# Attention's softmax within batches of 64 nodes, and attention and token mixing by 64x64 blocks of TensorE's array

## The reference, cut to what matters

```
layer 0:  agg = einsum('nm,bmd->bnd', A_hat, x);  two linear layers with batch norm
layer 1:  xp  = einsum('mn,bnf->bmf', L_norm, x);  h = relu(layernorm(xp @ Wc + bc)) + x
          q, k, v: 4 heads of 64;  scores = q k^T / 8, where(adj > 0, scores, -1e9)
          o = softmax(scores) @ v;  layernorm(x1 + o @ Wo);  MLP of 512 with gelu
layer 2:  h = relu(einsum('ts,bsh->bth', adj, x @ Wg0 + bg0));  h = relu(einsum(..., h @ Wg1 + bg1))
          then LSTMs over windows of 1 to 4 nodes (10 cells)
layer 3:  graph attention, softmax over the nodes of a batch
```

## Time and profile before

| | us |
|---|---|
| median of 3 runs | 2272.82 (2272.42 to 2273.76) |
| profiled execution | 2277.71 |
| its span | 2275.9 |
| PE busy | 2078.6 (91%) |
| DVE busy | 1650.3 (73%) |
| ACT busy | 1363.2 (60%) |
| POOL busy | 201.5 (9%) |

### The profile page before, as it was taken

The page is one execution under the profiler, slowest core; times in us unless marked ns, Lnnn a source line. Parts: engine busy times, 40 slices in busy tenths (PEclk is TensorE's granted clock), DMA queues, the critical chain, the costliest instruction groups (busy, mean ns, idle before and its releaser), DMA issues.

```text
span 2275.9 us, 56395 instructions
## 1 busy us (share of the span) xinstructions
PE 2078.6 (91%) x21545; PEld 1786.0 (78%) x21545; DVE 1650.3 (73%) x4811; ACT 1363.2 (60%) x3393; POOL 201.5 (9%) x260
## 2 busy tenths in 40 slices
PE   7989669999899999999999989999999999999986
PEld 4544358889788988888888978898889888888875
DVE  5769556777777777777677877777777777777744
ACT  5547335666565756666566656575657566666653
POOL 2000010010101010101010110001010101010100
PEclk9989779999999999999999999999999999999997
DMA  7747200000100001000100010001000010000000
GB/s 272 268 168 270 78 10 11 11 11 2 39 2 20 2 2 40 11 11 2 40 11 11 2 39 11 11 2 32 10 11 11 2 40 11 11 2 11 2 11 10
DMA packets 36751, 86.39 MB, mean 38 GB/s; under 512 B 2416, under 2 KB 26992, under 8 KB 32752
## 3 DMA queue, kind: packets, MB, share of 16 engines
q1 hardware_dynamic: 36464, 82.56, 10.4%
HBM read 52.15 MB, written 30.41 MB: 36 GB/s over the span
## 4 chain that ended last, share of the span: by engine, by line
PE 33%; DVE 22%; issue 19%; ACT 10%; POOL 5%; DVEq 0%; ACTq 0%; POOLq 0%
PE ps L257 9%; PE ps L258 9%; PE ps L259 9%; POOL rstd L1505 5%; DVE stats L1546 3%; ACT pool_mem L1379 2%; DVE pool_mem L1692 2%; ACT pool_mem L1413 2%; DVE pool_mem L1676 1%; PE ps L1092 1%; DVE pool_mem L1678 1%; ACT pool_mem L1421 1%; DVE mv L1550 1%; DVE hl_a L1598 1%; DVE hl_b L1598 1%
## 5 line engine op out<-in xcount | busy, mean ns | idle before, releaser
L1413 ACT ACTIVATE pool_mem<-ps,lstm_b 128x128 f32<-128x128 f32 (+2 forms) x1248 | 438.1, 415 | 289.8 <-PE ps L259 273.3
L257 PE MATMUL ps<-hl_a,w_hi 128*128 128x256 f16 (+2 forms) x1984 | 469.8, 260 | 21.7 <-DVE hl_a L776 8.0
L258 PE MATMUL ps<-hl_a,w_hi 128*128 128x256 f16 (+2 forms) x1984 | 469.2, 260 | 0.0
L259 PE MATMUL ps<-hl_a,w_lo 128*128 128x256 f16 (+2 forms) x1984 | 469.2, 260 | 0.0
L257 PE MATMUL ps<-hl_b,w_hi 128*128 128x168 f16 (+2 forms) x1408 | 361.9, 265 | 21.3 <-issue 17.0
L258 PE MATMUL ps<-hl_b,w_hi 128*128 128x168 f16 (+2 forms) x1408 | 361.4, 265 | 0.0
L259 PE MATMUL ps<-hl_b,w_lo 128*128 128x168 f16 (+2 forms) x1408 | 360.9, 265 | 0.0
L1505 POOL TENSOR_TENSOR rstd<-ve,nhalf 128x2 f32<-128x2 f32 x224 | 184.2, 825 | 1834.9 <-DVE ve L1553 1834.9
L257 PE MATMUL ps<-pool_mem,w_hi 128*128 128x128 f16 (+2 forms) x1536 | 313.0, 234 | 0.7
L258 PE MATMUL ps<-pool_mem,w_hi 128*128 128x128 f16 (+2 forms) x1536 | 312.9, 234 | 0.0
L259 PE MATMUL ps<-pool_mem,w_lo 128*128 128x128 f16 (+2 forms) x1536 | 312.8, 234 | 0.0
(11 more groups left out here) (246 smaller groups left out, 4587.4 us busy)
## 6 DMA issues: line engine op xcount, KB each, us to landing
xa<-in_x SPq DMA_DIRECT2D x32, 512.0 KB, 4.8
h_scratch<-pool_mem SPq DMA_DIRECT2D x14, 1024.0 KB, 4.2
pool_mem<-h_scratch SPq DMA_DIRECT2D x14, 1024.0 KB, 6.4
pool_mem<-in_wpack SPq DMA_DIRECT2D x16, 704.0 KB, 4.1
out<-xb SPq DMA_DIRECT2D x16, 512.0 KB, 2.9
o_scratch<-act_in SPq DMA_DIRECT2D x14, 512.0 KB, 3.2
act_in<-o_scratch SPq DMA_DIRECT2D x14, 512.0 KB, 5.6
row<-in_rows SPq DMA_DIRECT2D x1, 1408.0 KB, 10.2
```

The costliest lines, as they stand in the source:

```text
L257: nc.tensor.matmul(o, l[0], r[0], start=first, stop=False, skip_group_check=True)
L258: nc.tensor.matmul(o, l[0], r[1], start=False, stop=False, skip_group_check=True)
L259: return nc.tensor.matmul(o, l[1], r[0], start=False, stop=last, skip_group_check=True)
L1413: op = nc.scalar.activation(gates[s][:, g, m * w:(m + 1) * w], ps[s][:, g, m * w:(m + 1) * w], ACT.Tanh, bias=lstm_b[:, bias:bias + 1], sc ...
```

## The change

1. Softmax is computed within a batch only. The mask is 128x64. The scores of a half are 16 matmuls of 64x64x64 that use the two diagonal quadrants of the array (partitions 0 to 63 into 0 to 63, 64 to 127 into 64 to 127) and fill one bank. DVE adds the mask, takes the minimum of each row and subtracts it in three operations of 512 columns; ACT takes one exponential; DVE sums, inverts and scales. There are 4 transposes and one copy.
2. Attend is 16 matmuls of 64x64x64 in all four quadrants of the array, one bank for each batch of a block.
3. `mix` and `aggregate` go through a new function `quarters`: instead of one matmul with a block-diagonal matrix, four with its 64x64 block, in the four quadrants, one bank for each batch. ACT's and DVE's splits read two banks through a view; the number of elements is the same.
4. Banks: the gcn's first product moves to another bank, and the second one waits for the low half of half 0 too.
The list of the round is not changed, nor is the order of the steps on any engine. `pe.sem_inc(begun, 1)` is a semaphore increment on PE ahead of each such group.

```diff
+        def quarters(to, of, matrix):
+            for f in range(KT):
+                for c in (slice(0, P // 2), slice(P // 2, P)):
+                    for batch in range(P // NODES):
+                        n = slice(batch * NODES, (batch + 1) * NODES)
+                        mm = nc.tensor.matmul(to(f, batch)[c, :], of(f)[n, c], matrix[n, n], start=True, stop=True)
+            return mm
...
-                nc.gpsimd.tensor_scalar(mask1[:, :], a_bd[:, :], 0.0, MASK_L1, ALU.is_le, ALU.mult).then_inc(set_ok, 1)
+                for b in range(P // NODES):
+                    pool.wait_ge(set_ok, b + 1)
+                    d = slice(b * NODES, (b + 1) * NODES)
+                    nc.gpsimd.tensor_scalar(mask1[d, :], a_bd[d, d], 0.0, MASK_L1, ALU.is_le, ALU.mult).then_inc(set_ok, 1)
...
                 def aggregate(s, n):
-                    for f in range(KT):
-                        for b in range(BLK):
-                            mm = nc.tensor.matmul(ps[s][:, f, b * P:(b + 1) * P], xa[s][:, b, f * P:(f + 1) * P],
-                                                  gcn_t[:, :], start=True, stop=True)
+                    pe.sem_inc(begun, 1)
+                    for b in range(BLK):
+                        mm = quarters(lambda f, batch: ps[s][:, batch, (f * BLK + b) * NODES:(f * BLK + b + 1) * NODES],
+                                      lambda f: xa[s][:, b, f * P:(f + 1) * P], gcn_t)
...
+            MIX_BANK = {"o": [(0, 1), (2, 3)], "xp": [(0, 1), (2, 3)], "m0": [(0, 1), (2, 3)], "m1": [(0, 1), (2, 3)]}
...
                 def mix(s, n, h, src, matrix, which):
-                    bank = FEAT_BANK[which][h]
-                    for f in range(KT):
-                        for b in range(HALF):
-                            mm = nc.tensor.matmul(fea(s, bank)[:, f, b * P:(b + 1) * P],
-                                                  src[s][:, h * HALF + b, f * P:(f + 1) * P], matrix[:, :],
-                                                  start=True, stop=True)
+                    banks = MIX_BANK[which][h]
+                    pe.sem_inc(begun, 1)
+                    for b in range(HALF):
+                        mm = quarters(lambda f, batch: ps[s][:, banks[batch], (f * HALF + b) * NODES:(f * HALF + b + 1) * NODES],
+                                      lambda f: src[s][:, h * HALF + b, f * P:(f + 1) * P], matrix)
...
                 def scores(s, n, h):
                     pe.wait_ge(*taken.at(s, n, h, "k"))
+                    pe.sem_inc(begun, 1)
+                    to = scores_of(s, h)
                     for b in range(HALF):
-                        for head in range(HEADS):
-                            d = slice(head % 2 * HEAD_DIM, head % 2 * HEAD_DIM + HEAD_DIM)
-                            mm = nc.tensor.matmul(score(s, h, b, head), q[s][h][d, head // 2, b * P:(b + 1) * P],
-                                                  kk[s][h][d, head // 2, b * P:(b + 1) * P], start=True, stop=True)
+                        for pair in range(PAIRS):
+                            for batch in range(BATCHES):
+                                at_b = b * P + batch * NODES
+                                for odd in range(2):
+                                    d = slice(odd * HEAD_DIM, (odd + 1) * HEAD_DIM)
+                                    mm = nc.tensor.matmul(to[d, (b * PAIRS + pair) * BATCHES + batch, :],
+                                                          q[s][h][d, pair, at_b:at_b + NODES],
+                                                          kk[s][h][d, pair, at_b:at_b + NODES], start=True, stop=True)
...
                 def turn_probs(s, n, h):
+                    pe.wait_ge(*prob_ok.at(s, n, h, "scaled"))
+                    for b in range(HALF):
+                        for pair in range(PAIRS):
+                            c = (b * PAIRS + pair) * P
+                            mm = nc.tensor.transpose(ps[s][:, BANK_A[h], c:c + P], prob[s][h][:, b, pair, :], ident[:, :])
...
                 def attend(s, n, h):
+                    pe.sem_inc(begun, 1)
+                    banks = MIX_BANK["o"][h]
+                    for b in range(HALF):
+                        for pair in range(PAIRS):
+                            for odd in range(2):
+                                for batch in range(BATCHES):
+                                    d = slice(odd * HEAD_DIM, (odd + 1) * HEAD_DIM)
+                                    k = slice(batch * NODES, (batch + 1) * NODES)
+                                    c, head = (pair * HALF + b) * NODES, 2 * pair + odd
+                                    mm = nc.tensor.matmul(ps[s][d, banks[batch], c:c + NODES],
+                                                          vv[s][h][k, b, head * HEAD_DIM:(head + 1) * HEAD_DIM],
+                                                          prob_tr[s][h][k, b, pair, odd * NODES:(odd + 1) * NODES],
+                                                          start=True, stop=True)
...
                 def gcn_second(s, n, h):
+                    pe.wait_ge(*feat_lo.at(s, n, 0, "m1"))
                     pe.wait_ge(*feat_lo.at(s, n, h, "m1"))
...
                 def exps(s, n, h):
+                    act.wait_ge(*smax_ok.at(s, n, h, "shifted"))
+                    nc.scalar.activation(probs_of(s, h), probs_of(s, h), ACT.Exp, scale=-1.0).then_inc(soft_ok.of(s, h), 1)
...
                 def mask_scores(s, n, h):
+                    p = probs_of(s, h)
+                    dve.wait_ge(*attn_ps.at(s, n, h, "scores"))
+                    nc.vector.tensor_tensor(p, scores_of(s, h), mask1[:, :].unsqueeze(1).broadcast_to([P, SETS, NODES]), ALU.add)\
+                        .then_inc(smax_ok.of(s, h), 1)
+                    dve.wait_ge(*smax_ok.at(s, n, h, "masked"))
+                    nc.vector.tensor_reduce(smin[s][:, h * SETS:(h + 1) * SETS], p, AX.X, ALU.min).then_inc(smax_ok.of(s, h), 1)
+                    dve.wait_ge(*smax_ok.at(s, n, h, "least"))
+                    nc.vector.tensor_tensor(p, p, by_set(smin, s, h), ALU.subtract).then_inc(smax_ok.of(s, h), 1)
...
                 def invert_sums(s, n, h):
+                    nc.vector.reduce_sum(ssum[s][:, i], p, axis=AX.X).then_inc(smax_ok.of(s, h), 1)
+                    dve.wait_ge(*smax_ok.at(s, n, h, "sums"))
+                    nc.vector.reciprocal(ssum[s][:, i], ssum[s][:, i]).then_inc(smax_ok.of(s, h), 1)
+                    dve.wait_ge(*smax_ok.at(s, n, h, "inverse"))
+                    nc.vector.tensor_tensor(p, p, by_set(ssum, s, h), ALU.mult).then_inc(prob_ok.of(s, h), 1)
```

More of the change, by code:

```diff
@@ L927, in build @@
             pre_ok = Signal("pre_ok", "xa")
-            prob_ok = Signal("prob_ok", "b0 b1")
+            prob_ok = Signal("prob_ok", "scaled")
             ln_rstd = Signal("ln_rstd", " ".join(NORMS))
@@ L979, in fea, with feat, like_feat, scores_of @@
                 return ps[s][:, bank, :].rearrange("p (k n) -> p k n", k=KT)
+            def feat(s, h, which):
+                if which in MIX_BANK:
+                    first, second = MIX_BANK[which][h]
+                    return ps[s][:, first:second + 1:second - first, 0:HTOK].rearrange("p c (k b n) -> p k b c n", k=KT, b=HALF)
+                return fea(s, FEAT_BANK[which][h])
+            def like_feat(buf, which):
+                return buf.rearrange("p k (b c n) -> p k b c n", b=HALF, n=NODES) if which in MIX_BANK else buf
             def half_row(name):
                 return row[:, ROWS.index(name), :].unsqueeze(1).broadcast_to([P, HALF, DIM])
-            def score(s, h, b, head):
-                c = (b * 2 + head // 2) * P
-                return ps[s][:, (BANK_A, BANK_B)[head % 2][h], c:c + P]
+            PAIRS = HEADS // 2
+            BATCHES = P // NODES
+            SETS = HALF * PAIRS * BATCHES
+            def scores_of(s, h):
+                return ps[s][:, BANK_B[h], :].rearrange("p (j k) -> p j k", j=SETS)
+            def probs_of(s, h):
+                return prob[s][h].rearrange("p b c j -> p (b c j)").rearrange("p (j k) -> p j k", j=SETS)
+            def by_set(buf, s, h):
+                return buf[s][:, h * SETS:(h + 1) * SETS].unsqueeze(2).broadcast_to([P, SETS, NODES])
             mem = pool_mem
@@ L1348, in high @@
                 def high(s, n, h, which):
-                    src = fea(s, FEAT_BANK[which][h])
+                    src = feat(s, h, which)
                     act.wait_ge(*feat_ps.at(s, n, h, which))
@@ L1612, in mask_scores @@
                 def mask_scores(s, n, h):
-                    wait_apart(*attn_ps.at(s, n, h, "scores"))
-                    for b in range(HALF):
-                        for head in range(HEADS):
-                            i = (h * HALF + b) * HEADS + head
-                            op = nc.vector.tensor_tensor_reduce(prob[s][h][:, b, head, :], score(s, h, b, head), mask1[:, :],
```

(2 more changed lines are left out.)

90 lines of the change are left out of this document (32 added, 58 removed).

## The result

| | before | after |
|---|---|---|
| median, runs side by side (us) | 2272.62 (2268.16 to 2275.1) | 2251.44 (2248.24 to 2262.8) |
| ratio, 95% interval | | 0.9916 [0.9892, 0.994] |
| profiled span | 2275.9 | 2253.2 |

What follows compares the result with a forecast made beforehand. PE was taken as the bound: 61.5 us off it, less 15.2 lost to waits, plus 1 for ACT, less 2 for code, gave 45; 2277.7 became 2232.7, adjusted to the median 2228 us. Range 2200 to 2268.

Steps and rivals of the forecast that it cites:

- Prices: PE group costs read from the trace: a mix 0.89 us, scores 1.09, attend 1.03, a shape switch 0.10.
- The change on PE: Mixes, attend, scores, transposes and aggregate in quadrants, at 0.056 us a pass, take 61.5 us off PE.
- A: PE records have a floor of 0.025 us, so mixes lose 15; about -5 us, 2268; chance 0.11.
- B: Only two of PE's four quadrants run at once; +9 to +10 us, 2282; chance 0.10 with worse.
- C: Scores' row halves pay for sharing one bank: 2.04 us a group, 28 more in all, 2256; chance 0.05.
- The change on DVE and ACT: Softmax: DVE stays about 3.6 us a half, reductions 0.69, chain from 5.08 to 4.5 us.
- ACT's relief: Fewer exponentials and copies on ACT save 2.5 us and a copy a half; valued 0 to 8, taken as 1.
- What of it arrives: Of PE's 61.5 us saving, 15.2 is lost in groups ahead of waits for other engines.
- attend's saving: Attend gets 0.40 us shorter, 12.8 in all; 3.2 counted lost, at the odd stream's half 1 only.
- Rival D: ACT's and DVE's chains of the cell set the pace; 15 to 25 us more lost, 2243 to 2253; chance 0.15.
- the 94%: PE's figure in the steady window, cited as evidence against ACT's and DVE's chains setting the pace.
- Rival E: First phase's loop, with twice the PE instructions, stalls on code; 20 us more, 2248; chance 0.04.

Runs made afterwards that it cites:

- agg_only: The kernel before with only the first phase's aggregate in quadrants; 2265.36 us, ratio 0.9962 [0.9948, 0.9976] to before.
- fill_open: The changed kernel plus unread products ahead of attn_out half 1, the last layer's turn_att and six waits of stream 0's opening; 2229.69 us, ratio 0.9822 to before.
- before_shift: The kernel before with 13 semaphore increments on PE, run once ahead of the loop over rounds; 2290.39 us, ratio 1.0078 to before.

## Why the prediction was wrong in size

- **Prices, and "The change on PE"**: right. 61.5 us was the sum; work fell by 65.6. Passes of 0.059, scores at 1.08: rivals A, B and C are out. The two rules of the Trainium skill's "TensorEngine Tiling (Array Packing)" that stood beside A and C (Instruction Overhead, Gotcha 1) did not hold for f32 products in four quadrants and for row tiles that write different partitions of one bank: 32 records of a mix take 0.62, where at 0.025 each they would take 0.80, and 32 records of scores take 1.08 in one bank, where rival C's sum for two row tiles in turn gave 2.04.
- **"The change on DVE and ACT"**: right. Chain 4.47; reductions 0.69; ACT's relief brought nothing.
- **"What of it arrives"** failed: this is the step that made the forecast wrong. It let 15.2 of 61.5 go; in fact 40.2 went to waits and 3.0 to the clock. For the aggregate 6.3 was forecast to arrive, and `agg_only` is 8.4 faster there; but work less waits gave only 4.0 of it (12.2 less 8.2), and 4.4 came from the clock, so that the number fits by luck. The miss is in the rest: a loss of 8.9 was put down, and waits took 31.8 and the clock 8.9. I charged only groups that stand directly ahead of a wait. But at the place shown above the wait ends with a chain on ACT and DVE, the cell's, that begins before the group and did not become shorter (3.24 us in both): whatever shrinks between its start and its end goes, whichever group it is, with transposes between or not. That the other places where waits grew are of the same kind is argued from the list, not shown one by one. I counted attend's saving as lost for the odd stream alone; the place shown is the other stream's, counted as won. And I had no term for the clock, although before already spent 48.6 us in it.
- **Rival D** (0.15, 2243 to 2253) named the main cause and held the time; the clock wasn't in it. Its evidence, four of five waits for ACT or DVE, weighed more than the 94% that I set against it.
- **Rival E** named the wrong loop. The first phase got no issue wait of that size; the loop over rounds has it, and its size hangs on the place of the code. That before and after both fell on places that cost little (36 and 167) was chance, which the forecast had no part in: 13 instructions more made before 18 us slower.

## What to carry to other kernels

When PE waits in each half for a chain that began before the work you shorten, take the whole chain's length from the trace (start of its first step to PE's resumption) and count the saving only where PE arrives later than its end. Where waits of about 2 us stay, look at the clock, and try to fill them with products that nobody reads: it won 22 us here, as much as the change. In the kernel before the same kind of filling won nothing, though there the place of the code moved too, so measure it. And before a loss of 0.5% in a program with a long loop is put down to the edit, move its code by some instructions and time it again.

## What the runs showed of the hardware

- Four 64x64 f32 passes in the four quadrants start 6 to 7 ns apart and repeat every 58 to 59 ns; the array's change of shape adds about 0.09 us on either side.
- Behind a wait of about 2 us the granted clock can be 0.50 for 3.4 us (19 of the 27 low stretches in after are that long), and can stay at 1.00. All low stretches together are 78 us in `fill_open`, 155 in after, 148 in before.
- Behind a branch back PE waits 2.5 to 3.4 us in before (17.0 in six laps). A boundary in PE's code 4 to 25 instructions behind the landing brings a second wait of 0.6 to 3.1 in each lap. Clock goes with it: 0.9648 on average in `before_shift`, 0.9702 in before. That boundaries come every 256 instructions is a fit to the programs, borne out by the two kernels that were moved away from one.
- Semaphore increments in a row on PE, run once ahead of the loop, make a gap that grows with their number: 1.0 us with 13, 1.5 with 16, 2.5 with 22, 5.2 and 5.4 with 40.
- A row-wise reduction of 128x512 to 128x8 on DVE takes 0.686 us, as a two-input pass does.
